# One transformer layer on one core: the order of score pairs and value products in the attention loop

## The reference

```python
Q, K, V = X @ Wq + bq, X @ Wk + bk, X @ Wv + bv          # split into 16 heads
attn = softmax(einsum('bhqd,bhkd->bhqk', q, k) / sqrt(16))
out = einsum('bhqk,bhkd->bhqd', attn, v) @ Wo + bo
x = layernorm(X + out)
gate, up = silu((x @ w_gate) * s_gate), (x @ w_up) * s_up   # int8 weights, 256 x 1024
x = layernorm(x + ((gate * up) @ w_down) * s_down)
```

## Time and profile before

| what | value |
|---|---|
| median of 3 runs | 595.54 us (595.34 to 595.89) |
| the profiled execution | 596.11 us |
| its span, first to last instruction | 594.1 us |
| ScalarE (ACT), busy | 505.2 us, 85% of the span |
| VectorE (DVE), busy | 459.2 us, 77% |
| GpSimd (POOL), busy | 47.4 us, 8% |
| granted TensorE clock, mean | 0.998 of full |

### The profile page before, as it was taken

How to read it: one execution, slowest core, us unless ns; L and a number is a source line. 1 busy time by engine, 2 the same in 40 slices (tenths; PEclk the granted TensorE clock), 3 DMA queues, 4 the chain that set the end, 5 groups by cost and what they waited for, 6 DMA issues and landing times.

```text
span 594.1 us, 10873 instructions
## 1 busy us (share of the span) xinstructions
PE 584.3 (98%) x4096; PEld 247.8 (42%) x4096; DVE 459.2 (77%) x836; ACT 505.2 (85%) x614; POOL 47.4 (8%) x47
## 2 busy tenths in 40 slices
PE   8999999999999999999999999999999999999995
PEld 7884222222222223223222322222222227988875
DVE  6678888989888867687686668888868696686875
ACT  4539999999999999999999999999999995163352
POOL 6600000000000000000000000003000001102023
PEclk9999999999999999999999999999999999999999
DMA  9466948212303020111211010111010000101102
GB/s 219 61 107 84 126 63 105 29 26 35 86 11 70 8 34 9 31 15 26 62 16 29 11 30 11 30 46 32 9 32 7 7 5 8 41 1 36 36 1 71
DMA packets 36185, 24.72 MB, mean 42 GB/s; under 512 B 24930, under 2 KB 30946, under 8 KB 35538
## 3 DMA queue, kind: packets, MB, share of 16 engines
q1 hardware_dynamic: 34740, 23.29, 23.0%
q10 hardware_dynamic: 1392, 0.72, 0.5%
HBM read 6.56 MB, written 4.33 MB: 18 GB/s over the span
## 4 chain that ended last, share of the span: by engine, by line
PE 97%; DVE 1%; DMA 0%; issue 0%; ACT 0%; POOL 0%; POOLq 0%
PE ps L1289 42%; PE ps L1261 29%; PE ps L1362 10%; PE ps L1131 6%; PE ps L1394 5%; PE ps L1316 2%; PE ps L1102 1%; DVE attn_q L834 1%; PE ps L1336 1%; PE ps L1117 1%; PE ps L1319 1%; DMA out<-out_tmp 0%; DVE xt_lo L736 0%; PE ps L1163 0%; DVE neg_mean L1076 0%
## 5 line engine op out<-in xcount | busy, mean ns | idle before, releaser
L668 ACT ACTIVATE probs<-ps 128x1024 f32<-128x1024 f32 (+1 forms) x512 | 442.9, 1093 | 12.0 <-PE ps L1261 11.6
L1289 PE MATMUL ps<-probs,v_all 128*17 128x512 f32 x1910 | 268.9, 598 | 0.9
L1261 PE MATMUL ps<-q_slot,k_stack 51*128 51x512 f32 x1024 | 196.4, 456 | 0.0
L1261 PEld LDWEIGHTS ps<-q_slot,k_stack 51*128 51x128 f32 x1024 | 84.4, 184 | 219.2 <-ACT probs L668 204.6
L908 DVE TENSOR_SCALAR bits<-ps 128x512 int32<-128x512 f32 x69 | 47.5, 689 | 32.6 <-PE ps L1261 31.3
L1289 PE MATMUL ps<-poly,v_all 128*17 128x512 f32 x138 | 71.3, 598 | 0.0
L687 ACT ACTIVATE sg<-ps,sgate_c 128x512 f32<-128x512 f32 x32 | 22.0, 688 | 49.3 <-PE ps L1362 49.3
L1289 PEld LDWEIGHTS ps<-probs,v_all 128*17 128x17 f32 x1910 | 33.6, 95 | 59.9 <-issue 45.8
L932 DVE SCALAR_TENSOR_TENSOR poly<-poly,bits 128x512 f32<-128x512 f32 x69 | 49.3, 714 | 7.2
L928 DVE SCALAR_TENSOR_TENSOR poly<-poly,mant 128x512 f32<-128x512 f32 x69 | 47.7, 692 | 2.4
L919 DVE SCALAR_TENSOR_TENSOR poly<-mant 128x512 f32<-128x512 f32 x69 | 47.2, 684 | 0.0
(11 more groups left out here) (101 smaller groups left out, 447.9 us busy)
## 6 DMA issues: line engine op xcount, KB each, us to landing
q_slot<-qy SPq DMA_DIRECT2D x64, 64.0 KB
k_stack<-k_part SPq DMA_DIRECT2D x12, 256.0 KB
at_dram<-attn_q SPq DMA_DIRECT2D x64, 34.0 KB
at<-at_dram SPq DMA_DIRECT2D x8, 272.0 KB, 2.9
q_slot<-qy SPq DMA_DIRECT2D x64, 32.0 KB
x_tok<-in_L_attn_X SPq DMA_DIRECT2D x14, 128.0 KB, 5.6
k_stack<-k_part SPq DMA_DIRECT2D x12, 128.0 KB
out<-out_tmp SPq DMA_DIRECT2D x12, 128.0 KB, 2.2
```

What stands on the lines that cost most here:

```text
L668: nc.scalar.activation(probs[:, slot_of(g), first:2, :].rearrange("p a b -> p (a b)"), ps[:, 2 * ring + first:2 * ring + 2, :].rearrange(" ...
L1261: last = nc.tensor.matmul(ps[:, 2 * ring + half, :], k_stack[s % QUADS][base:base + ROWS, p, kt * P:(kt + 1) * P], q_slot[slot][base:base ...
L1289: last = nc.tensor.matmul(ps[32 * hh:32 * hh + VW, ACC, :], v_all[:, tiles[hh], NQ * (s % QUADS) + hh, :], prob, start=(kt == 0), stop=(kt ...
```

## The change

In TensorE's order the first score pair of unit 0 stands alone at the start. From then on a group holds the second pair of a unit, the first pair of the next unit, and the value products of the unit before in place of those two before. The last unit's group has one pair and no value products. VectorE's tiles in steps 0 to 4 are 1, 4, 7, 10 and 13 in place of 2, 5, 8, 11 and 14, and their places in the order of value products are 4, 7, 10, 13 and 15 as before. In the other steps tiles and places stay.

```diff
         def poly_tiles(s):
-            return [2, 5, 8, 11, 14] if s <= QUADS else [2, 6, 10, 13]
+            return [1, 4, 7, 10, 13] if s <= QUADS else [2, 6, 10, 13]

         def value_order(s):
-            behind = ({2: 4, 5: 7, 8: 10, 11: 13, 14: 15} if len(poly_tiles(s)) == 5 else {2: 5, 6: 9, 10: 12, 13: 15})
+            behind = ({1: 4, 4: 7, 7: 10, 10: 13, 13: 15} if len(poly_tiles(s)) == 5 else {2: 5, 6: 9, 10: 12, 13: 15})
...
             UNITS = UPS * STEPS
+            scores(0)
             for u in range(UNITS):
-                scores(2 * u)
                 scores(2 * u + 1)
+                if u + 1 < UNITS:
+                    scores(2 * u + 2)
                 if u < 2:
                     project_v(V_LATE + u)
-                if u >= 2:
-                    prob_times_v(u - 2)
+                if 1 <= u < UNITS - 1:
+                    prob_times_v(u - 1)
```

## The result

The changed kernel takes 666.86 us in the median of four runs (666.42 to 668.74), the kernel before 595.47: a ratio of 1.12 (1.1187 to 1.1213). It is 71 us slower where 3 had been forecast.

What follows compares the result with a forecast made beforehand. ScalarE was taken to set the pace, never starved in five-tile steps, only at projections and turns in four-tile steps. Terms +2.0 + 1.1 + 0.3 - 0.4 = +3.0 gave 598.5 us against the median 595.54; range 597.2 to 599.9.

Steps and rivals of the forecast that it cites:

- Rival A: Whole kernel: TensorE's own pace counts, stalls only change places, start and tail stay; +0.7 us, 596.2; chance 0.15.
- B: Step 12: GpSimd's cast catches two VectorE operations, value products wait 2.7 us; 600.6 in all; chance 0.08.
- C: Attention loop: the ring does not hold a group's second pair, so all twelve projection stalls go; 591.5 us; chance 0.10.
- the echo: Behind projection stalls at tiles 8 and 15: groups with a half exponential stall ScalarE again; bound 0 if not there.
- Point 1: Attention loop: value products u-1 need exponential 2u-1, which scores 2u+2 ahead of them already wait for; cost 0.
- point 3: Five-tile steps 1 to 4: smallest slack 0.23 in either order; cost 0, without VectorE's margin up to 1.2 us.
- the walk of ring and slack: Attention loop: reckoning from ring-held score pairs how much TensorE can lose before ScalarE starves; smallest slack 0.23 in five-tile steps.
- Point 4: Start of the loop: scores 5 wait for VectorE's first tile, TensorE idle 0.47; +1.1 us, bounds 0 and 1.6.
- Point 5: Step 12: GpSimd's cast slows VectorE's last operation of a tile, so value products wait; +0.3 us, bounds 0 and 0.7.
- the toss: Step 12: VectorE's operation starts within 0.1 us of GpSimd's cast, so whether it is held is open; 0 or 0.7.
- Point 6: Tail: the last value products go before scores 511, so gate_up(0) starts sooner; -0.4 us, bounds -0.5 and 0.
- Point 2: Four-tile steps, at projections and turns: a half exponential is now second of its group; +2.0 us, bounds 0 and +2.6.

Runs made afterwards that it cites:

- a faster kernel: The kernel before with each output projection of the first three chunks cut in two halves, spread over tiles 8, 15, 1 and 3: 594.07 us, ratio 0.996.
- 618.65: The changed kernel with VectorE's tiles in steps 0 to 4 back at 2, 5, 8, 11, 14 and their old places: 618.65 us, ratio 1.038.
- 619.19: The changed kernel with VectorE's tiles 1, 4, 7, 10, 13 used at products 3, 6, 9, 12, 15: 619.19 us, ratio 1.039.
- the filled kernel: The changed kernel with twelve unused transposes ahead of four value products in each of steps 1 to 4: 653.47 us, ratio 1.0966.

## Why the prediction was wrong

**What bounds the kernel** was right. The tiles' removal cost 26.5 us against 29.6 less 2.5 reckoned, and a faster kernel came from the account of slack and stalls. Rival A is refuted by that run: had TensorE set the pace, it would have stayed under 600. Rivals B and C did not appear. The stated range of 597.2 to 599.9 does not follow from the bounds of its terms: they give 597.4 with the start at its lower end, 596.5 with the echo at its, and 600.4 with all at the upper ones. 666.86 is far outside either way.

**Point 1, new waits, failed,** at the sentence "Value products u-1 need exponential 2u-1 ... Cost 0". It holds for heads 1 to 3. The sentence read the loop and not the operands: head 0's tile is `ORDER[s][kt]`, and the order of tiles was in the diff, with the places of VectorE's tiles. I used these places to ask whether VectorE's results are in time, and never what stands in the places between. The runs put about 23 us in its stead for one tile ahead (618.65 and 619.19 against 595.89), and 47.7 more where two tiles ahead meet one unit behind, of which the filled kernel gives back 13.4 as the cost of the low clock.

**The new waits interact with point 3.** "Steps 1 to 4 cost 0, at most 1.2" came out at 44.8. No run contradicts the walk of ring and slack itself: without tiles such a step lasts 29.33 us in the new loop and 29.36 in the old. In the changed kernel scores wait for VectorE's first tile at no step but the first. But the walk started from a value product that waits for nothing. No rival carried this case, though "nothing can be won in five-tile steps" is no statement on what can be lost there.

**The low clock** was in no term. The rows before show 0.998 throughout, and a stop of TensorE of 1.8 us, four times a step, did not occur there.

**Point 4, the start,** was right in place, and in size partly by luck. Scores 5 wait for VectorE:

```profile
49.81 0.33 PEld L1261 LDWEIGHTS ps<-q_slot,k_stack 51*128 51x128 f32 x4 [1.38 <-ACT probs L668]
49.84 0.73 PE L1261 MATMUL ps<-q_slot,k_stack 51*128 51x512 f32 x4 [0.49 <-DVE bits L908]
```

Idle 0.49 against the 0.47 forecast, at 49.84 against 50.04. Exponential 5 ends at 51.40, 0.20 sooner than forecast, and exponential 9 at 54.92, where 54.89 had been forecast: a new wait of about 0.2 lies between the two.

**Point 5, step 12,** did not happen. In the changed kernel the cast starts at 471.56, when VectorE has ended the last operation of that tile (471.53). The schedule had moved, so the toss was not tested.

**Point 6, the tail,** was not there. TensorE starts `gate_up(0)` 1.28 us before the last exponential ends (560.25 and 561.53), before 1.23 (489.47 and 490.70). The gain is 0.05 and not 0.4: value products 253 wait for an exponential too (one tile ahead). They begin 0.89 behind their scores and not 0.66, which eats 0.23 of the lead; the rest is not traced.

**Point 2, the pairing and its echo,** can't be read apart in the changed kernel, because a wait of point 1 stands at every VectorE tile. The two kernels without tiles differ by 0.86 us within their uncertainty, and have no halves. So the +2.0 stays untested.

## What to carry to other kernels

When a consumer is moved closer to its producer, list for each operand of each instruction which item it reads, and take the largest distance ahead; one operand in four on another order is enough. In this kernel a look-ahead of a tiles with a distance of d units cost nothing at (1, 2), 0.25 to 0.28 us a time at (1, 1), 0.82 at (2, 2) and 1.7 at (2, 1) with the clock at full: the two parts of a change that cost 23 and 22 us alone cost 71 together, the low clock included. Before adding work to a gap of an engine that feeds the bottleneck, compare it with the slack and with what one period gives back, and cut it to fit.

## What the runs showed of the hardware

TensorE's clock fell although its matmul row never stood idle for more than 1.8 us at a time within the loop: with such stops four times in 38 us the granted clock of steps 1 to 4 was 0.87 to 0.91, a mean between its two levels of 1.2 and 2.4 GHz. In step 1 it stood at 0.50, the lower level, three times for about 3 us. The first time was right behind the stop that ended at 92.34, and the eight matmuls there took 1.91 us in place of 1.05. Behind the stop that ended at 100.61 it stayed at 1.00. With the stops of the two-ahead products filled by transposes it was 1.00. In the kernel with the tiles alone, whose stops are 0.9 us, and 1.07 once a step, it stayed at 1.00:

```profile
79.42:110.92 31.50, 26.89 (x194) 7.04 (x194) 23.37 (x41) 28.06 (x33) 0.00 (x0) 1.00 0.51 70
```

The fall cost 12.9 us in four steps, and nothing in the trace of the kernel before, at 0.998 throughout, had shown it.
